# Front of the second layer in a two-layer transformer block: earlier context loads, alternating batch steps, and the expert combination moved into the second product

## The reference, cut to what matters

```python
y = jnp.einsum('nec,ech->nh', combine, expert_out)
out = y + SHARED_SCALE * shared
...
def bitnet_linear(x, W, b):
    w_scale = jnp.maximum(jnp.mean(jnp.abs(W)), 1e-05)
    qW = jnp.sign(W) * (jnp.abs(W) > 0.5 * w_scale).astype(W.dtype)
    i_scale = jnp.maximum(jnp.max(jnp.abs(x)), 1e-08) / 127.0
    qx = jnp.clip(jnp.round(x / i_scale), -128.0, 127.0)
    out = jnp.einsum('...i,oi->...o', qx, qW) * (w_scale * i_scale)
    return out + b
...
vis = bitnet_linear(dinov2_features, W_d2v, b_d2v)
image_embeds = bitnet_linear(vis, W_img, b_img)
fused = bitnet_linear(text_embeddings, W_txt, b_txt)
```

## Time and profile before

| | us |
|---|---|
| median of 3 runs (1155.12 to 1157.1) | 1155.41 |
| the profiled execution, its own time | 1153.72 |
| span in its profile | 1151.9 |
| last quarter of expert 7 ends on DVE | 746.7 |
| first product's scale ready, second product's rounding begins | 801.2 |
| second product's scale ready, combination begins | 836.4 |
| normalization begins | 858.6 |
| attention's first matmul | 882.0 |

### The profile page before, as it was taken

How to read it: one execution, slowest core, us unless ns; L and a number is a source line. 1 busy time by engine, 2 the same in 40 slices (tenths; PEclk the granted TensorE clock), 3 DMA queues, 4 the chain that set the end, 5 groups by cost and what they waited for, 6 DMA issues and landing times.

```text
span 1151.9 us, 22949 instructions
## 1 busy us (share of the span) xinstructions
PE 830.1 (72%) x7974; PEld 620.2 (54%) x7974; DVE 753.4 (65%) x1496; ACT 576.0 (50%) x1226; POOL 322.8 (28%) x272
## 2 busy tenths in 40 slices
PE   4657768777777844899889999805515999565896
PEld 2335545554555533667767777702113777345895
DVE  8638556665568757667577767326696566677666
ACT  3325435444445422654365555238955555474463
POOL 3347555655557410447000000065000000013000
PEclk9568888888789965599999999957757788787898
DMA  5363545444664332434275663083000000002001
GB/s 139 81 118 86 122 94 113 107 115 102 130 108 95 76 101 75 149 116 142 81 219 152 192 183 116 32 206 76 0 8 1 1 1 0 1 1 73 2 0 58
DMA packets 83108, 99.95 MB, mean 87 GB/s; under 512 B 25475, under 2 KB 65965, under 8 KB 82966
## 3 DMA queue, kind: packets, MB, share of 16 engines
q1 hardware_dynamic: 77474, 90.35, 31.2%
q0 software_dynamic: 4096, 6.57, 2.2%
q10 hardware_dynamic: 1476, 2.20, 0.6%
HBM read 74.10 MB, written 13.32 MB: 76 GB/s over the span
## 4 chain that ended last, share of the span: by engine, by line
PE 43%; DVE 14%; DMA 13%; SPq 12%; ACT 7%; issue 6%; POOL 3%; ACTq 1%; DVEq 0%; POOLq 0%
PE ps L1124 10%; PE ps L1111 8%; DMA qs<-mTl 5%; SPq L434 4%; SPq L431 4%; PE ps L1628 3%; PE ps L1876 2%; DMA area<-in_ctxT_dram 2%; PE ps L542 2%; ACT area L1740 2%; PE ps L1617 2%; PE ps L1887 2%; PE ps L1622 2%; PE ps L375 1%; PE ps L1707 1%
## 5 line engine op out<-in xcount | busy, mean ns | idle before, releaser
L529 DVE TENSOR_REDUCE m<-ps 100x2 f32<-100x722 f32 x128 | 114.6, 899 | 104.9 <-PE ps L524 104.1
L549 ACT ACTIVATE p<-ps 121x600 f32<-121x600 f32 x128 | 85.5, 668 | 104.4 <-PE ps L542 102.5
L542 PE MATMUL ps<-qs,ks 128*121 128x100 f16 x768 | 75.3, 242 | 69.8 <-DMA qs<-mTl 64.4
L1465 POOL PARTITION_ALL_REDUCE gmax<-cmax x6 | 6.2, 1039 | 410.3 <-DVE cmax L1460 410.3
L542 PEld LDWEIGHTS ps<-qs,ks 128*121 128x121 f16 x768 | 66.7, 157 | 87.3 <-DMA qs<-mTl 43.5
L1173 ACT ACTIVATE hT<-ps,cols 128x500 f32<-128x500 f32 (+1 forms) x96 | 62.5, 652 | 99.2 <-PE ps L1111 99.0
L1124 PE MATMUL ps<-w_h,hT_h 128*125 128x256 f16 (+1 forms) x384 | 104.7, 273 | 1.8 <-DVE x L1219 1.2
L1124 PE MATMUL ps<-w_h,hT_l 128*125 128x256 f16 (+1 forms) x384 | 104.7, 273 | 0.0
L1124 PE MATMUL ps<-w_l,hT_h 128*125 128x256 f16 (+1 forms) x384 | 104.7, 273 | 0.0
L564 DVE SCALAR_TENSOR_TENSOR p<-p,xe 121x600 f32<-121x600 f32 x128 | 101.4, 793 | 2.3 <-DMA xe<-floor 2.0
L1180 DVE TENSOR_TENSOR hT_l<-hT,hT_h 128x500 f16<-128x500 f32 (+1 forms) x96 | 61.3, 641 | 61.3 <-ACT hT_h L1174 61.3
(11 more groups left out here) (362 smaller groups left out, 2434.5 us busy)
## 6 DMA issues: line engine op xcount, KB each, us to landing
xe<-floor SPq DMA_DIRECT2D x32, 378.1 KB
ks<-kp SPq DMA_DIRECT2D x96, 90.8 KB
sw<-in_L_ffn_w_dram SPq DMA_DIRECT2D x16, 512.0 KB, 7.0
sw<-in_L_ffn_w_dram SPq DMA_DIRECT2D x8, 1024.0 KB, 5.7
stage<-in_L_xattn_W_f_dram SPq DMA_DIRECT2D x6, 1024.0 KB, 7.0
ctx_f<-in_ctxT_dram SPq DMA_DIRECT2D x16, 270.8 KB, 6.3
stage<-in_ctxT_dram SPq DMA_DIRECT2D x8, 541.5 KB, 8.6
area<-in_ctxT_dram SPq DMA_DIRECT2D x4, 1083.0 KB, 15.5
```

The source lines that it names most:

```text
L529: v.tensor_reduce(m32[p][:, 2 * i:2 * i + 2], ps[0:T, at:at + 2, 0:KV], AX.X, ALU.max).then_inc(m_max, 1)
L542: mm = pe.matmul(bank[t_bank(i) + n][0:KT, j * T:(j + 1) * T], ks[p][:, h, j * KT:(j + 1) * KT], qs[p][:, h, :], start=(j == 0), stop=True ...
L549: s.activation(p32[:, i % HALF, :, :, :].rearrange("p j n t -> p n j t"), ps[0:KT, t_bank(i):t_bank(i) + 2, 0:KJ * T].rearrange("p n (j t) ...
```

## The change

- SP: a new `early_context` stands in the block of expert 6, ahead of that expert's store. It waits for three things that free the memory (last expert's rows turned, its first and second weights split) and loads the context of batches 0 to 7 with 8 transfers. `layer2_loads` now waits for expert 6's buffer alone and loads batches 8 to 15 with 8 transfers. `ctx_f` and `vis_f` lie batch by batch in memory, and `b2` is placed behind `zeros`, out of the way of the early batches.
- DVE: the context's scale is computed in the last block ahead of expert 7's output quarters and not behind them. ACT rounds batches 0 to 7 of the context directly after its last expert work.
- First and second product: DVE rounds batch b and takes the maximum of batch b-2 in turn; ACT evicts batch b and rounds ahead in turn. The loops are written out.
- `combine_vector(v, i)` is now one step of a pipeline: the statistics of earlier batches, the second row of batch i-1, the first row of batch i. One such step stands behind each batch of the second product.
- The third rounding is divided: on ACT 4 batches ahead of the transposed copies, 5 behind them, 7 between the text evictions; on DVE 4 behind the normalization, 5 behind the text maximum, 7 behind the text rounding.

```diff
-        b2 = [sbb(f"b2_{p}", [CT, C]) for p in range(2)]
         xe = [sbb(f"xe{p}", [CT, 4, C]) for p in range(2)]
         zeros = sbb("zeros", [CT, 4, C])
+        b2 = [sbb(f"b2_{p}", [CT, C]) for p in range(2)]
...
+            if not has_block(n, 1):
+                quant_scale(v, CTX, [(D2V, D2V)])
...
         def layer2_scalar(s):
+            def round_context(b):
+                s.wait_ge(c_ctx_in[b // 4], 16 * 4)
+                round_scalar(s, CTX, ctx_f, KC, b)
+
             s.wait_ge(q_scale, CTX + 1)
+            for b in range(B // 2):
+                round_context(b)
             for b in range(B):
...
+                if b == B // 2 - 1:
+                    s.wait_ge(ys_out[1], 16 * E)
+                lin_scalar(s, 0, vis_f, oscale[:, D2V:D2V + 1], col("L1_xattn_b_d2v"), False, b)
+                if b == B // 2 - 1:
+                    round_context(b + 1)
+                    round_context(b + 2)
+                elif B // 2 <= b < B - 2:
+                    round_context(b + 2)
+            s.wait_ge(q_scale, VIS + 1)
+            for b in range(B + 2):
+                if b < B:
+                    round_scalar(s, VIS, vis_f, 128, b)
+                if b >= 2:
+                    lin_scalar(s, 1, img_f, oscale[:, IMG:IMG + 1], col("L1_xattn_b_img"), True, b - 2)
...
+                if B // 2 + 1 + n < B:
+                    round_scalar(s, IMG_, img_f, 128, B // 2 + 1 + n)
...
+        def combine_vector(v, i):
+
+            if i > 0:
+                vs.sync(v)
+            if i >= 3 and i - 3 < B:
+                last = v.bn_aggr(meanvar[:, i - 3, :], stats[:, i - 3, :])
+            if i >= 2 and i - 2 < B:
+                last = v.bn_stats(stats[:, i - 2, :], x[:, i - 2, :])
+            if i >= 1 and i - 1 < B:
+                last = v.scalar_tensor_tensor(x[:, i - 1, :], pick(1, i - 1), weight[1][:, i - 1:i], x[:, i - 1, :],
+                                              ALU.mult, ALU.add)
+            if i < B:
+                v.wait_ge(got[i // 2], 64)
+                last = v.scalar_tensor_tensor(x[:, i, :], pick(0, i), weight[0][:, i:i + 1], x[:, i, :],
+                                              ALU.mult, ALU.add)
+            vs.inc(last)
...
+            for b in range(B + 2):
+                if b < B:
+                    round_vector(v, 1, vis_f, vis_q, b)
+                if b >= 2:
+                    lin_max_vector(v, 1, img_f, b - 2)
+                combine_vector(v, b)
...
+        def early_context(sp):
+
+            sp.wait_ge(x_t, CC * E)
+            sp.wait_ge(w1_l, 2 * (E + 1))
+            sp.wait_ge(w2_s, 2 * (E + 1))
+            for b in range(B // 2):
+                sp.dma_start(ctx_f[:, b, :, :], ctx_d[b]).then_inc(c_ctx_in[b // 4], 16)
+
         def layer2_loads(sp):
 
-            for p in range(2):
-                sp.wait_ge(ys_out[p], 16 * E)
-            ctx_all = a["ctxT"].rearrange("(c p) n -> p c n", c=2)
-            for i in range(B // 4):
-                at = slice(i * 4 * KV, (i + 1) * 4 * KV)
-                sp.dma_start(ctx_f[:, :, at], ctx_all[:, :, at]).then_inc(c_ctx_in[i], 16)
+            sp.wait_ge(ys_out[0], 16 * E)
+            for b in range(B // 2, B):
+                sp.dma_start(ctx_f[:, b, :, :], ctx_d[b]).then_inc(c_ctx_in[b // 4], 16)
...
                 first_load(sp, e + 3, 0)
+                if not has_block(n, 2) and has_block(n, 1):
+                    early_context(sp)
                 if not is_shared(n):
                     expert_store(sp, e, p)
```

More of the change, by code:

```diff
@@ L1550, in run, with batch_of, round_scalar, round_vector @@
                 body(i, i // step, i % step)
[L1553 to L1566, removed]
+        def batch_of(src, b):
+            return src[:, b, :, :] if len(src.shape) == 4 else src[:, :, b * KV:(b + 1) * KV]
+        def round_scalar(s, k, src, rows_, b):
+            v = batch_of(src, b)
+            s.activation(v, v, ACT.Copy, scale=iinv[0:rows_, k:k + 1], bias=MAGIC).then_inc(c_p1, 1)
+        def round_vector(v, n, src, dst, b):
+            v.wait_ge(c_p1, B * n + b + 1)
+            v.tensor_scalar(dst[:, :, b * KV:(b + 1) * KV], batch_of(src, b), -MAGIC, None, ALU.add).then_inc(c_q, 1)
         def lin_tensor(pe, n, w, src):
@@ L1577, in lin_tensor, with lin_scalar, lin_max_vector @@
             run(pe, B, 2, 0, 2, body)
[L1579 to L1594, removed]
+        def lin_scalar(s, n, dst, scale, bias, sums, b):
+            for c in range(CC):
+                s.wait_ge(c_mm, 2 * (B * n + b) + c + 1)
+                kw = {"accum_out": avg_sum[:, c, b:b + 1]} if sums else {}
+                s.activation(batch_of(dst, b)[:, c, :], bank[2 * (b % 2) + c][:, 0:KV], ACT.Identity,
+                             scale=scale, bias=bias[:, c:c + 1], **kw).then_inc(c_ev, 1)
+        def lin_max_vector(v, n, dst, b):
+            v.wait_ge(c_ev, 2 * (B * n + b) + 2)
+            v.tensor_reduce(pmax[:, b:b + 1], batch_of(dst, b), AX.XY, ALU.max, apply_absolute_value=True
+                            ).then_inc(c_pm, 1)
         def att_tensor(pe):
@@ L1713, in layer2_scalar @@
         def layer2_scalar(s):
+            def round_context(b):
+                s.wait_ge(c_ctx_in[b // 4], 16 * 4)
+                round_scalar(s, CTX, ctx_f, KC, b)
             s.wait_ge(q_scale, CTX + 1)
+            for b in range(B // 2):
+                round_context(b)
             for b in range(B):
[L1716 to L1724, removed]
+                if b == B // 2 - 1:
[12 more added lines that the diff above has]
+                    lin_scalar(s, 1, img_f, oscale[:, IMG:IMG + 1], col("L1_xattn_b_img"), True, b - 2)
+            s.wait_ge(ln_var, LG + 2)
+            s.activation(stddev[:, :], vareps[:, :], ACT.Sqrt).then_inc(ln_std, 1)
+            s.wait_ge(q_scale, IMG_ + 1)
+            for b in range(4):
+                round_scalar(s, IMG_, img_f, 128, b)
+            for n in range(B // 2):
+                s.wait_ge(ln_tr, 2 * (B // 2) + n + 1)
+                s.copy(xnT[:, :, n * 2 * T:(n + 1) * 2 * T].rearrange("p c (b t) -> p c b t", b=2),
+                       bank[n][:, 0:4 * T].rearrange("p (c b t) -> p c b t", c=CC, b=2)).then_inc(ln_ev, 1)
+            for b in range(4, B // 2 + 1):
+                round_scalar(s, IMG_, img_f, 128, b)
             s.wait_ge(q_scale, TEXT + 1)
@@ L1763, in layer2_vector @@
         def layer2_vector(v):
             vs.sync(v)
-            lin_round_vector(v, 0, ctx_f, ctx_q)
-            lin_max_vector(v, 0, vis_f)
+            v.wait_ge(f_y, 4 * NB)
+            for b in range(B + 2):
+                if b < B:
+                    round_vector(v, 0, ctx_f, ctx_q, b)
+                if b >= 2:
+                    lin_max_vector(v, 0, vis_f, b - 2)
+            v.wait_ge(c_pm, B)
             quant_max(v, VIS, B)
             quant_scale(v, VIS, [(IMG, IMG)])
-            lin_round_vector(v, 1, vis_f, vis_q)
@@ L1771, in layer2_vector @@
-            lin_max_vector(v, 1, img_f)
+            for b in range(B + 2):
+                if b < B:
+                    round_vector(v, 1, vis_f, vis_q, b)
+                if b >= 2:
+                    lin_max_vector(v, 1, img_f, b - 2)
+                combine_vector(v, b)
+            v.wait_ge(c_pm, 2 * B)
             quant_max(v, IMG_, B)
+            combine_vector(v, B + 2)
+            vs.sync(v)
+            v.tensor_scalar(vareps[:, :], meanvar[:, :, 1], LN_EPS, None, ALU.add).then_inc(ln_var, 1)
@@ L1773, in layer2_vector @@
             vs.inc(v.tensor_scalar(avg[:, :, :], avg_sum[:, :, :], 1.0 / KV, None, ALU.mult))
+            v.memset(lmax[:, :], 0.0).then_inc(x_moe, 1)
             quant_scale(v, IMG_, [(ATT, ATT), (ATT + 1, ATT + 1)])
-            combine_vector(v)
-            v.wait_ge(x_moe, 1)
-            ln_vector(v, 2)
+            v.wait_ge(ln_std, LG + 2)
+            vs.inc(v.reciprocal(rstd[:, :], stddev[:, :]))
+            vs.sync(v)
+            for b in range(B):
+                v.tensor_scalar(xn[:, b, :], x[:, b, :], meanvar[:, b, 0:1], rstd[:, b:b + 1],
+                                ALU.subtract, ALU.mult).then_inc(ln_xn, 1)
@@ L1779, in layer2_vector @@
+            for b in range(4):
+                round_vector(v, 2, img_f, img_q, b)
             v.wait_ge(ln_ev, 3 * (B // 2))
@@ L1784, in layer2_vector @@
             v.tensor_scalar(txt_q[:, :, :], xnT[:, :, :], -MAGIC, None, ALU.add).then_inc(h_q2, 1)
-            lin_round_vector(v, 2, img_f, img_q)
+            for b in range(B // 2 + 1, B):
+                round_vector(v, 2, img_f, img_q, b)
             for q in range(Q):
```

5 lines of the change are left out of this document (2 added, 3 removed).

## The result

The changed kernel takes 1146.55 us in the median of 14 runs, the kernel before beside it 1154.81; the ratio is 0.9924 (95% interval 0.9899 to 0.995). It is faster, by 0.8% or 8.8 us (by the ratio; the two medians are 8.3 apart) and not by 31. Single executions of the changed kernel lie between 1142.9 and 1154.6. The profiled execution took 1145.13 us, its span is 1143.3.

The account below looks back on a forecast made before the run. ACT was taken to bound the second product and DVE the combination, behind waits for context loads. Gains 24.0 + (56.7 - 42.3) - 0.4 - 6.6 = 31.4 us gave 1124.0 us from the median 1155.4, range 1119 to 1134.

Parts of the forecast that it names:

- The scale takes 1.3 us as before (799.86 to 801.16): Between first and second product: the scale again takes 1.3 us, so ACT begins the second product at 777.2 us.
- First product: With context loaded early and rounded beside expert 7, it ends at 775.9 us against 799.9 before: 24.0 us gained.
- rival D: Early load held back by one of its waits or the store's transfers; first product from 745 us, time 1127; chance 0.05.
- Second product with combination: DVE becomes the bound at 2.48 us per batch; the stage takes 42.3 us instead of 56.7.
- rival B: Second product: alternating on DVE isn't free, costing 6 us or at most 11.5; time 1130 to 1135.5; chance 0.17.
- Text part: Normalization to attention: third roundings now stand in the path, giving back 6.6 us; attention starts 30.0 us behind the normalization.
- Rival A: First product: contexts of the second half land late beside gathers, ACT waits 6 us, time 1130; chance 0.13.
- The Trainium skill's rule on queues taking turns: DMA engines alternate between queues by packets of descriptors, so shorter descriptors would cost the context its share against the gathers.
- Rival C: Combination: gathers starve and DVE waits for their rows; slower than before, 1165 at 3.0 us per gather; chance 0.03.
- rival C's rule: Such DVE instructions lock GpSimd out of the port pair it writes descriptors by; trace showed 0.30 us at most.
- the distance from there to the end 269.9 us as before: From the attention's start to the end no instruction is changed, so that part keeps its length of 269.9 us.
- the prediction's own sign: The forecast is wrong if the part behind the attention's start changes its length by more than 1 us.

Follow-up runs that it names:

- e1: Changed kernel with the reduction for the first product's scale moved in POOL's list behind the 16th of 32 gathers, not the last; 1125.2 us, ratio 0.9741.
- e8: e1 with the third rounding's batches placed elsewhere on ACT and DVE, where those had idle time around the text rounding and scale; 1119.6 us, ratio 0.9668.
- e3: Changed kernel with the reduction for the first product's scale ahead of all 32 gathers in POOL's list; 1141.9 us, ratio 0.9884.
- e2: Kernel before with the reduction for the first product's scale moved behind the 16th gather in POOL's list; 1154.3 us, ratio 0.9997.
- e9: Changed kernel, POOL's list as changed, with the third rounding placed as in e8; 1139.4 us, ratio 0.9839.
- e11: Kernel before with nothing moved, only the batch loops of roundings, evictions and maxima on ACT and DVE written out; 1157.1 us, ratio 1.0011.
- e7: e1 with the combination and its statistics behind the second product's last maximum; 1140.3 us, ratio 0.9847.
- e5: Changed kernel without the early context load, all 16 transfers behind both expert stores; 1146.4 us, ratio 0.9896.
- e6: e1 without the early context load, all 16 transfers behind both expert stores; 1148.6 us, ratio 0.9913.

## Why the prediction was wrong

The direction held, the size did not: 31.4 us were forecast, 8.8 measured.

**The step that failed** is in the second product: "The scale takes 1.3 us as before (799.86 to 801.16)". That is DVE, POOL, DVE, and the 1.3 us held only because POOL was done with its gathers 3 us earlier. In the changed kernel the same step took 22.2 us, from the last maximum (776.37 + 0.91) to ACT's first rounding at 799.48. I moved the first product's end from 799.9 to 775.9 and left the gathers at 753.8 to 796.8, with both numbers in hand, and never laid POOL's list beside the new time. The wait that came in (21.56 us, less the 0.5 us it took before) is the miss: 102.8 in e1 plus 21.0 is the changed kernel's 123.8, and 1.7 of the 21.0 come from the gathers starting later (the last section), which the forecast had put at nothing. Without it the front would have been 102.8 us where I worked out 850.6 - 746.3 = 104.3, and the time 1125.2 where I forecast 1124.0.

The other steps, by their own numbers, in us behind the start of the last expert row:

- First product: maximum ready 29.6 forecast, 30.3 measured. The rows of ACT in the changed kernel, the first eight roundings and those of batches 8 and 9:

```profile
737.21 6.41 ACT L1561 ACTIVATE area<-area,iinv 96x722 f32<-96x722 f32 x8 [2.86 <-DVE oscale L1455]
...
759.44 1.68 ACT L1561 ACTIVATE area<-area,iinv 96x722 f32<-96x722 f32 x2 [0.85 <-DMA area<-in_ctxT_dram]
```

  The eight early batches are rounded beside expert 7 and wait for no transfer, so rival D is out. ACT waits 0.85 us for the context in all, against under 3.
- Second product with combination: DVE is the bound, 2.44 us for each batch against 2.48; from the scale to the normalization 42.2 us in e1 (73.4 - 31.2) against 43.4. DVE is busy 33.69 of 33.69 us from 803.31 to 837.00 in the changed kernel. Alternating on DVE cost nothing: rival B is out, and so is its upper bound. ACT had 5.2 us of idle time in it in e1 (34.35 of 39.53 us busy), where about 7 were forecast.
- Text part: from the normalization to the attention 29.4 us in e1 against 30.0, the text evictions 1.36 us apart against 1.4. That it gives back a part is right, and e8 takes most of it again.
- Rival A, contexts late: 0.85 us in place of 6. The Trainium skill's rule on queues taking turns (DMA: Bandwidth & Descriptors, Queues, rings and completion order; the prediction names another section of that page) had spoken for it. Batches 8 to 11 were there at 759.4 us, 12.5 us behind the last expert row where the forecast had 12.2, so the gathers took no share that mattered here; no run shows the rule by itself.
- Rival C was in the wrong place by one step. I asked whether gathers hold up DVE's combination, in the transfers; they held up the scale, in POOL's own list. e3 shows C's mechanism where the gathers come late, at 11.0 us.
- Of rival C's rule (the Trainium skill, SBUF — State Buffer, SBUF: two separate sides) e1 shows a trace: where gathers run beside the combination, the 16 issues from 781.07 on are 1.50 us apart and single ones take up to 1.58 us. The last 16 of the changed kernel, with DVE idle, are 1.31 us apart and take 1.01 us each. It is real, small, and hidden here; which of DVE's instructions does it wasn't tried.
- "the distance from there to the end 269.9 us as before" was wrong: it is 272.5 in the changed kernel. In the profiled executions this takes 2.6 us of the gain, and by the prediction's own sign (more than 1 us) it is a second miss; its cause is open.

## What to carry to other kernels

When a stage is made to end earlier, go through every queue that its next step passes, also the one with the 0.3 us instruction, and ask what stands ahead of that instruction at the new time; an order that cost nothing may have been covered by the lateness just removed. A wait that the profile ascribes to a fast instruction on another engine, where that engine shows no wait itself, was here a place in a list. And two parts of a change can hide each other: the early load measured alone was worth 0 us or 20.3 us, depending on one line of POOL's list.

## What the runs showed beyond that

The part behind the attention's start has the same instructions in all kernels, but took 269.9 and 270.0 us in before and e2, and 270.0 to 275.7 in the others (e9 270.0, e11 271.4, changed 272.5, e3 275.7, e7 275.4). Each figure is from one execution, while the time of one and the same kernel differs by up to 11.8 us between executions (e8), so what follows is observed and not shown to be caused.

From the last layer normalization to the end it took 101.1 and 101.2 us in before and e2 and 101.7 to 102.8 in all others, e11 among them, in which only loops are written out. So code outside of this part may shift it by about 1 us. Of the changed kernel's 2.6 us, 1.3 lie there; 0.8 lie in the attention (104.4 us from its first matmul to the next scale's maximum, 103.6 before) and 0.6 between the two. The further 3.2 us of e3 lie in the attention alone, with the PE clock: 107.6 us at 0.82 granted, against 104.4 at 0.85 in the changed kernel.

At the attention's start the changed kernel's PE runs at 1.2 GHz for over 4 us (0.50 granted from 870.81 to 874.40), before it for 2.5 us. PE had stood idle for 5.71 us ahead of it, behind the last text eviction, and for 2.69 us before. The thirteen traces fall into two groups by this idle time: behind 5.7 to 7.0 us (eight kernels) the part takes 271.4 to 275.7 us, behind 1.0 to 2.7 us (before, e2, e8, e9, e11) 269.9 to 271.6; in e9, with 1.01 us, PE starts at 2.4 GHz. e3 and the changed kernel start alike, so the start alone doesn't make the difference between those two. e11 was expected at 272 us if the code's layout decides and at 270 if the clock does; its 271.4 decides neither. What makes the difference between the kernels stays open.

The transfers of batches 8 to 15, issued right behind expert 7's store, took SP 6.37 us for the eight issues against 3.79 us for the eight early ones, and that store took 7.71 us to complete instead of 6.04; the first gather was 9.1 us behind the last expert row instead of 7.5. The store's piece in the chain of the changed kernel, then of e5, where the loads wait until it is done:

```profile
747.45 7.71 DMA slots_out<-ye
```

```profile
745.03 6.05 DMA slots_out<-ye
```

e1 has 7.70 us with the loads right behind the store, e6 6.10 without them: the loads behind it are what slows the store. In the changed kernel this adds to the wait for POOL, in e1 it is hidden.
